# First cross-attention: denominators summed one step later from a deeper fold buffer, other work moved to other steps

## The chip, the cores and the metric

The kernel runs on one core of one Trainium2 chip. The metric is the device time of one execution in microseconds. Before the change it is 1993.03 us, the median of three runs (1991.8 to 1994.41).

The core has engines that run their own queues in order and wait for each other by semaphores: TensorE (PE; its weight loads are PEld), VectorE (DVE), ScalarE (ACT), GpSimd (POOL) and SyncE (SP, which here issues the transfers).

## The reference, cut to what matters

Two layers, each a gated cross-attention and a gated feed-forward part, over x of 4 batches x 1024 tokens x 256 and a context of 4 x 77 x 256. All the edits are in the first of the four stages:

```python
x = x + jnp.tanh(g_xattn[0]) * _L0_xattn_ref(_layernorm(x, axis=-1), ctx_1024, ctx_1024, wq, bq, wk, bk, wv, bv, wo, bo)

def _L0_xattn_ref(q, k, v, wq, bq, wk, bk, wv, bv, wo, bo):   # 16 heads of 16
    qh = (q @ wq.T + bq) ...; kh = (k @ wk.T + bk) ...; vh = (v @ wv.T + bv) ...
    attn = softmax(einsum('bhqd,bhkd->bhqk', qh * SCALE, kh), axis=-1)
    out = einsum('bhqk,bhkd->bhqd', attn, vh)
    return out.reshape(B, Nq, C) @ wo.T + bo
```

The later stages (ternary feed-forward, second cross-attention, self-attention with top-3 gating) are the same code before and after.

## The kernel before

`first_attention` works on tiles of 128 tokens. There are 32 of them (T) and 16 pairs (n, two tiles), four pairs to a batch. Every engine walks through the same list of steps, `for T in STEPS` with T from -12 to 34, and in each step issues its share in an order written out by hand. Nothing else sets the order: an engine that waits holds back all that it has still to issue.

For a tile the work passes through the engines so:

- TensorE, step T-2: scores (L414), after the shift of the tile before it has read them.
- VectorE, step T-2: negative row maximum (L754, `row_max`) and shift (L769, `shift`).
- ScalarE, step T-2: exponential (L564, `exp`), in odd steps behind the evacuation of a query (L528).
- GpSimd, step T-2: `fold` adds each row of probabilities in three halvings, `half_sum` (L624), `quarter` (L626), `eighth` (L630). `eighth` has two buffers; the third halving waits for VectorE's reciprocal of two tiles before.
- VectorE, step T-1: `recip_sum` adds the ten numbers that remain per head (L776) and takes the reciprocal (L777). It waits for `eighth` of its tile.
- GpSimd, step T: `widen` copies the reciprocals to the width of a head, two copies (L639), ring of four (`r_wide`).
- TensorE, step T: transposes of the probabilities (L425) in groups of 4, 4 and 2.

Two tiles on, in odd step 2n+1, TensorE transposes the widened reciprocals of pair n-1 (`reciprocals`, L400), when `widen` has been done 2n times (tiles 0 to 2n-1), and the residual of an earlier pair is done (`d_fin`). It does this behind the scores and the first group of transposes of the step. Behind it in the same step come the other two groups, the query projection (L385), the output matmuls of pair n-1, second half (L445), and in steps 3, 11 and 19 keys and values of the next batch (L341, L349). In even steps TensorE does the scores, the transposes, those of x (L373), the output matmuls of the first half (L445) and the output projection (L462). ScalarE evacuates the transposed reciprocals (L570), VectorE multiplies the outputs by them (`weigh`, L762) in the next even step and later adds the residual (L790).

GpSimd has more in its queue, in this order in step T: at T % 8 == 0 the inverse square roots of the layer norm of the next batch (`root`, L609 to L98, 15 small instructions, each waited for), at T % 8 == 1 the offset (L617, L618), `fold(T + 2)`, `widen(T)`, in odd steps the output bias (`add_bias`, L647), at (T + 1) % 8 == 0 the V blocks (`block_v`, L659, five instructions), and, at the steps in `CHUNK_STEPS`, one of 22 pieces of the feed-forward weights, rounded (`round_chunk`, L652). VectorE collects the bits of the same piece in the same step (`mantissas`, L801). A piece's buffer (four of them) is filled again by SP when both are through with it; SP's loop asks for pieces by the same list. Ahead of its loop GpSimd made ones, waited for the V bias and the output bias from memory (`s_wide`), and multiplied to get the V bias over a whole tile (`vb_wide`, L685), which TensorE uses in step -1 (`v_bias`) and VectorE then in `whole_bias` (L783, L784).

Of the kernel before, what the change touches and what calls it, by code (L numbers as in the profile page):

```python
# [8 lines left out]
ALU = mybir.AluOpType  # L9
ACT = mybir.ActivationFunctionType  # L10
AX = mybir.AxisListType

P = 128
# [5 lines left out]
RSQRT_MAGIC = 0x5F3759DF  # L19
WCH = 1024  # L20
STAGE = 4
CHUNK_STEPS = (-5, -4, -2, -1, 1, 3, 4, 5, 6, 7, 9, 11, 12, 13, 15, 17, 19, 20, 21, 23, 25, 27)
MANTISSA = 0x7FFFFF


# [39 lines left out]
def spread(ap, dim, n):  # L65

    shape = list(ap.shape)
    shape[dim] = n
    return ap.broadcast_to(shape)
# [31 lines left out]
def first_attention(nc, ident, gates, gates_src, x_src, x_dst, ctxT, wqT, wkT, wvT, woT, bias, H, ffn, head, tag):  # L101

    B, _, S = ctxT.shape
    HD = wqT.shape[1]
    dh = HD // H
    C = HD // P
# [6 lines left out]
    HALF = -(-S2 // 8) * 4  # L113
# [5 lines left out]
    RS = 4  # L119
# [25 lines left out]
    with semaphores(nc, tag) as sem, ExitStack() as ctx:  # L145
        def sb(name, shape, dt=F32):
            return ctx.enter_context(nc.sbuf_tensor(f"{tag}_{name}", shape, dt))
# [9 lines left out]
        kbias = sb("kbias", [P, C])  # L157
        kb_masked = sb("kb_masked", [P, C, HR])
        vbias = sb("vbias", [P, C])
        ones = sb("ones", [P, P])  # L160
        vb_wide = sb("vb_wide", [P, C, P])
        obias = sb("obias", [P, D])
        kt = sb("kt", [P, 2, C, HR, S])
# [14 lines left out]
        prob_all = sb("prob", [P, PR, KC * P])  # L178
        half_sum = sb("half_sum", [P, H, HALF])
        quarter = sb("quarter", [P, H, HALF // 2])  # L180
        eighth = sb("eighth", [P, 2, H, HALF // 4])
        negmax = sb("negmax", [P, H])
        rsum = sb("rsum", [P, RS, H])
        r_wide = sb("r_wide", [P, RS, H, dh])
# [46 lines left out]
        def _(sp):  # L231
# [63 lines left out]
            store_v(0)  # L295
            for i in range(2, STAGE):
                load_chunk(i)
            for dst, src in ((vbias[:, :], bv.rearrange("(c p) -> p c", p=P)),
                             (obias[:, :], spread(bo.rearrange("(a n) -> a n", a=1), 0, P))):
                sp.dma_start(dst, src, allow_slow_non_contiguous=True).then_inc(s_wide, 16)  # L300
            load_w(3, wo, woT)
            load_x(PB + 2)
            load_x(PB + 3)
# [298 lines left out]
        def _(pool):  # L602
# [17 lines left out]
            def fold(T):  # L620
                pool.wait_ge(a_exp, T + 1)
                if T:
                    pool.wait_ge(p_eighth, T)
                own.step(pool.tensor_tensor(half_sum[:, :, 0:S2 // 2], prob[:, T % PR, :, 0:S2 // 2],  # L624
                                            prob[:, T % PR, :, S2 // 2:S2], ALU.add))
                own.step(pool.tensor_tensor(quarter[:, :, :], half_sum[:, :, 0:HALF // 2],  # L626
                                            half_sum[:, :, HALF // 2:HALF], ALU.add))
                if T >= 2:
                    pool.wait_ge(d_r, T - 1)
                pool.tensor_tensor(eighth[:, T % 2, :, :], quarter[:, :, 0:HALF // 4],  # L630
                                   quarter[:, :, HALF // 4:HALF // 2], ALU.add).then_inc(p_eighth, 1)

            def widen(T):
                pool.wait_ge(d_r, T + 1)
                if T >= RS:
                    pool.wait_ge(e_r, (T - RS) // 2 + 1)
                by_place = rsum[:, T % RS, :].rearrange("p (g c j) -> p c g j", c=C, j=HR)
                for c in range(C):
                    ins = pool.tensor_copy(r_wide[:, T % RS, HC * c:HC * (c + 1), :].rearrange("p (g j) w -> p g j w", j=HR),  # L639
                                           spread(by_place[:, c, :, :].unsqueeze(3), 3, dh))  # L640
                ins.then_inc(p_wide, 1)
# [37 lines left out]
                own.link(pool.affine_select(out=v_mask[:, i, :], in_=v_mask[:, i, :], compare_op=ALU.is_ge, fill=0.0,  # L679
                                            base=S - 1 - P * k + SEG * m, pattern=[[S2, HR]], channel_multiplier=-1))  # L680
            own.wait()
            own.step(pool.memset(ones[:, :], 1.0))
            pool.wait_ge(s_wide, 32)
            for c in range(C):
                ins = pool.tensor_tensor(vb_wide[:, c, :], ones[:, :], spread(vbias[:, c:c + 1], 1, P), ALU.mult)  # L685
            ins.then_inc(s_vb, 1)
            pool.wait_ge(s_pad, 1)
            pool.wait_ge(root_done, 1)
            for T in STEPS:
                n, odd = divmod(T, 2)  # L690
                if T % 8 == 0 and 1 <= (T + 8) // 8 <= B:
                    root((T + 8) // 8)
                if T % 8 == 1 and 1 <= (T + 8) // 8 <= B:
                    offset((T + 8) // 8)
                if 0 <= T + 2 < TILES:
                    fold(T + 2)
                if 0 <= T < TILES:
                    widen(T)
                if odd and 0 <= n < NP:
                    add_bias(n)  # L700
                if (T + 1) % 8 == 0 and 0 <= (T + 1) // 8 < B:
                    block_v((T + 1) // 8)
                if T in CHUNK_AT:
                    round_chunk(CHUNK_AT[T])

        @block.vector
        def _(dve):
# [64 lines left out]
            def recip_sum(T):  # L772
                dve.wait_ge(p_eighth, T + 1)
                if T >= RS:
                    dve.wait_ge(p_wide, T - RS + 1)
                own.step(dve.tensor_reduce(rsum[:, T % RS, :], eighth[:, T % 2, :, :], AX.X, ALU.add))  # L776
                dve.reciprocal(rsum[:, T % RS, :], rsum[:, T % RS, :]).then_inc(d_r, 1)  # L777

            def whole_bias():
# [46 lines left out]
            for T in STEPS:  # L826
                n, odd = divmod(T, 2)
                if not odd and 0 <= n - 2 < NP:
                    weigh(n - 2)
                if 0 <= T + 2 < TILES:  # L830
                    row_max(T + 2)
                if 0 <= T + 2 < TILES:
                    shift(T + 2)
                if 0 <= T + 1 < TILES:
                    recip_sum(T + 1)
                if T in CHUNK_AT:
                    mantissas(CHUNK_AT[T])
                if T == CHUNK_STEPS[-1] + 1:
                    mantissa_found()
                b, p = divmod(T + 12, 8)  # L840
                if p < PB and 0 <= PB * b + p < NP + HEAD:
                    ln_stats(PB * b + p)
                if T == -1:
                    whole_bias()
                if not odd and 0 <= n - 2 < NP:
                    residual(n - 2)
                if T == TILES:
                    judge()
# [1902 lines left out]
def laid_out(inputs):  # L2751

    import numpy as np

    def cols(v):
        return v.reshape(-1, P).T

    a = {}
    for name, v in inputs.items():
        v = np.asarray(v)  # L2760
        if name == "x":
            a[name] = v.reshape(-1, v.shape[-1])
        elif name == "ctx_1024":
            a["ctxT"] = v.transpose(0, 2, 1)
        elif name.startswith("L0_xattn_w") or (name.startswith("L0_ffn_") and name.endswith("_w")):
            a[name + "T"] = v.T
        elif name.endswith("Wkv"):
            half = v.shape[1] // 2
            a[name[:-3] + "Wk"], a[name[:-3] + "Wv"] = v[:, :half], v[:, half:]
        elif name in ("L0_xattn_bq", "L0_xattn_bk", "L1_xattn_ln_scale", "L1_xattn_ln_bias", "L0_ffn_w1_s",  # L2770
                      "L0_ffn_w2_s", "L0_ffn_h1_s", "L0_ffn_h2_s"):
            a[name] = cols(v)
        else:
            a[name] = v
    return {name: np.ascontiguousarray(v) for name, v in a.items()}
# [14 lines left out]
```

## Time and profile before

| what | value |
|---|---|
| profiled execution | 1992.12 us, span 1990.4 us from the first to the last instruction |
| median of three runs | 1993.03 us |
| mean granted TensorE clock | 0.978 |
| busy share of the span: PE, DVE, ACT, POOL | 93%, 60%, 55%, 37% |
| first attention | from 0 to about 250 us |
| the same shares from 175 to 200 us | PE 24.8, DVE 21.6, ACT 17.6, POOL 19.2 of 25 us |

Times in the rows are counted from the start of the span. L400 is line 400 of the kernel before. In a row of a timeline the first number is the start, the second the duration from there to the end of the last merged instruction, `x4` how many were merged, and the bracket how long the engine was idle before and what ended it. "issue" stands for idle time without a cause that the profile shows.

### The profile page before, as it was taken

How to read it: one execution, taken by the hardware profiler on the slowest of the kernel's cores; microseconds unless marked ns; L12 is line 12 of the kernel's file. 1: busy time of each engine (PE TensorE's matmuls, PEld its weight loads, DVE VectorE, ACT ScalarE, POOL GpSimd, SP SyncE). 2: the span in 40 equal slices, each digit the busy share in tenths (PEclk: the TensorE clock that was granted, in tenths of full speed). 3: DMA queues.
4: the chain of work that ended last, by engine and by line, in shares of the span. 5: the costliest groups of instructions: out<-in, count | busy, mean ns of one | idle time of the engine just before them, and what ended most of it. 6: DMA issues, size and time to landing. Idle time of an engine off the chain costs nothing. (4 is left out here: it accounts for less than half of the span.)

```text
span 1990.4 us, 60604 instructions
## 1 busy us (share of the span) xinstructions
PE 1845.3 (93%) x26589; PEld 1496.7 (75%) x26589; DVE 1184.3 (60%) x1654; ACT 1085.9 (55%) x1900; POOL 728.7 (37%) x1012
## 2 busy tenths in 40 slices
PE   6898779999999999998799987899999999999997
PEld 4666568787887878887678776788777887887875
DVE  7787522332323233242555543888888898888885
ACT  4666433443434344342455543677777777767763
POOL 6878601000010000000333331556655665656552
PEclk9999989999999999999799998999999999999999
DMA  5331000000000000000301004322332243223211
GB/s 178 99 101 56 23 27 1 22 21 1 22 1 22 22 1 22 0 22 12 110 28 44 30 22 118 87 66 63 93 104 58 60 109 93 61 62 109 78 51 35
DMA packets 147004, 106.23 MB, mean 53 GB/s; under 512 B 19992, under 2 KB 143152, under 8 KB 146736
## 3 DMA queue, kind: packets, MB, share of 16 engines
q1 hardware_dynamic: 146736, 102.28, 17.4%
q8 instruction: 215, 3.52, 0.7%
q14 instruction: 53, 0.43, 0.1%
HBM read 76.77 MB, written 25.49 MB: 51 GB/s over the span
## 5 line engine op out<-in xcount | busy, mean ns | idle before, releaser
L2264 ACT ACTIVATE E_prob<-E_ps_s,E_negmax 128x1024 f32<-128x1024 f32 x256 | 284.9, 1115 | 144.2 <-DVE E_negmax L2577 143.7
L2577 DVE TENSOR_REDUCE E_negmax<-E_ps_s 128x1 f32<-128x1024 f32 x256 | 301.4, 1219 | 82.6 <-PE E_ps_s L2084 82.2
L2584 DVE STREAM_TRANSPOSE E_prob<-E_prob 128x1024 f32<-128x1024 f32 x256 | 303.9, 1225 | 24.0 <-ACT E_prob L2264 11.5
L2103 PEld LDWEIGHTS E_ps_o<-E_prob,E_vrep 32*64 32x64 f32 x15872 | 231.1, 130 | 64.5 <-ACT E_part L2290 56.7
L2103 PE MATMUL E_ps_o<-E_prob,E_vrep 32*64 32x128 f32 x15872 | 262.5, 274 | 13.4 <-issue 3.9
L1690 ACT ACTIVATE F_raw<-F_ps,ffn_scales 128x512 f32<-128x512 f32 x128 | 88.3, 690 | 288.0 <-PE F_ps L1599 288.0
L1599 PE MATMUL F_ps<-F_ha,ffn_w_rounded 128*128 128x512 f32 x1024 | 240.7, 395 | 0.0
L1599 PE MATMUL F_ps<-F_hb,ffn_w_rounded 128*128 128x512 f32 x1024 | 240.2, 395 | 0.0
L1599 PEld LDWEIGHTS F_ps<-F_ha,ffn_w_rounded 128*128 128x128 f32 x1024 | 190.9, 188 | 48.4 <-issue 1.7
L1599 PEld LDWEIGHTS F_ps<-F_hb,ffn_w_rounded 128*128 128x128 f32 x1024 | 192.0, 188 | 46.9
L2480 POOL TENSOR_TENSOR E_part<-E_part 128x512 f32<-128x512 f32 x93 | 119.4, 1284 | 249.6 <-ACT E_part L2290 249.6
L1777 DVE TENSOR_TENSOR F_ha<-F_raw,F_ha 128x512 fp32r<-128x512 f32 x64 | 44.3, 692 | 184.2 <-ACT F_ha L1692 184.2
L1777 DVE TENSOR_TENSOR F_hb<-F_raw,F_hb 128x512 fp32r<-128x512 f32 x64 | 44.3, 692 | 169.2 <-ACT F_hb L1692 169.2
L1599 PE MATMUL F_ps<-F_xt_part,ffn_w_rounded 128*128 128x512 f32 x512 | 126.7, 407 | 10.7 <-POOL F_xt_part L1711 4.7
L95 POOL TENSOR_TENSOR F_rs<-F_rs 128x4 f32<-128x4 f32 x24 | 4.8, 199 | 337.5 <-DVE F_rs L1742 336.2
L2084 PE MATMUL E_ps_s<-E_k_hi,E_q_hi 64*128 64x512 f32 x512 | 114.4, 442 | 14.9 <-ACT E_prob L2264 13.5
L1599 PEld LDWEIGHTS F_ps<-F_xt_part,ffn_w_rounded 128*128 128x128 f32 x512 | 96.2, 194 | 39.0 <-DVE F_raw L1767 8.8
L1711 POOL TENSOR_TENSOR F_xt_part<-F_xt,F_xt_part 128x1024 fp32r<-128x1024 f32 x8 | 19.2, 2399 | 272.0 <-ACT F_xt_part L1658 163.9
L2084 PE MATMUL E_ps_s<-E_k_hi,E_q_lo 64*128 64x512 f32 x512 | 102.4, 393 | 0.0
L2084 PE MATMUL E_ps_s<-E_k_lo,E_q_hi 64*128 64x512 f32 x512 | 101.3, 390 | 0.0
L1767 DVE SCALAR_TENSOR_TENSOR F_raw<-F_ps,ffn_scales,F_silu 128x512 f32<-128x512 f32 x64 | 47.7, 750 | 67.7 <-ACT F_silu L1674 67.7
L2084 PEld LDWEIGHTS E_ps_s<-E_k_hi,E_q_hi 64*128 64x128 f32 x512 | 48.0, 184 | 42.6 <-ACT E_prob L2264 23.5
(315 smaller groups left out, 3912.7 us busy)
## 6 DMA issues: line engine op xcount, KB each, us to landing
E_vrep<-E_v_all SPq DMA_DIRECT2D x128, 256.0 KB, 3.0
A_w_stage<-in_L_ffn_h_wT SPq DMA_DIRECT2D x16, 512.0 KB, 3.9
E_v_all<-E_vst SPq DMA_DIRECT2D x32, 256.0 KB, 2.2
C_x<-x SPq DMA_DIRECT2D x20, 256.0 KB, 6.7
F_x<-x SPq DMA_DIRECT2D x9, 512.0 KB, 3.7
A_x<-in_x SPq DMA_DIRECT2D x16, 256.0 KB, 5.5
x<-A_x SPq DMA_DIRECT2D x16, 256.0 KB, 2.2
x<-F_x SPq DMA_DIRECT2D x8, 512.0 KB, 2.9
```

The lines of the kernel that those rows point to most:

```text
L95: own.step(eng.tensor_tensor(t, y, y, ALU.mult))
L1599: mm = pe.matmul(out, fw.chunk(w, name, k, j * P, (j + 1) * P), a[:, k, :], start=k == 0 and i == 0, stop=k == K - 1 and i == len(parts) - 1)
L1690: act.activation(raw[:, u % 2, :], ps[:, u % 4, :], ACT.Gelu, scale=scale).then_inc(u_raw, 1)
L1711: pool.tensor_tensor(xt_part[1][:, :, :], xt[:, :, :], xt_part[0][:, :, :], ALU.subtract).then_inc(xt_lo, 1)
L1767: dve.scalar_tensor_tensor(out=dst, in0=ps[:, 2 * (j % 2) + 1, :], scalar=scales[:, 1, j:j + 1], in1=silu[:, j % 2, :], op0=ALU.mult, op1= ...
L1777: dve.tensor_tensor(dst, raw[:, u % 2, :], hi, ALU.subtract).then_inc(u_lo, 1)
L2084: mm = pe.matmul(ps_s[:, j, keys], a[rows, c % 2, cols], k[rows, c % 2, keys], start=i == 0, stop=i == 2)
L2103: mm = pe.matmul(low[64 * j:64 * j + 64, g, :], vrep[rows, slot, KB // 4 * (quarter % 2) + k, dh * j:dh * (j + 1)], prob[rows, u % 2, :, j ...
L2264: act.activation(prob[:, s // UT % 2, s % UT, j, :], ps_s[:, j, :], ACT.Exp, bias=negmax[:, at:at + 1], scale=1.0, accum_out=den[:, 2 * c ...
L2480: pool.tensor_tensor(part[:, 0, :], part[:, 0, :], part[:, 1, :], ALU.add).then_inc(part_added, 1)
L2577: dve.tensor_reduce(negmax[:, at:at + 1], ps_s[:, j, :], AX.X, ALU.max, negate=True).then_inc(d_max, 1)
L2584: dve.transpose(at, at).then_inc(d_t, 1)
```

## The change

- `recip_sum(T)` is issued by VectorE in step T, it was in step T-1. `eighth` has three buffers and the third halving waits for the reciprocal of three tiles before.
- `widen(T - 1)` is issued by GpSimd in step T, it was `widen(T)`. TensorE's code, `reciprocals` included, is not in the diff.
- The V blocks are made at (T + 2) % 8 == 0, one step earlier.
- `CHUNK_STEPS` is a new list: after -5 and -4 come 1 to 6, 9 to 14, 18 to 22 and 26 to 28; steps -2, -1, 7, 15, 17, 23 and 25 have no piece any more.
- `whole_bias` is issued by VectorE in step 0 behind the maximum and the shift, it was at the end of step -1.
- `ones` is gone; the V bias is spread by copies in GpSimd's step -3, and the wait for `s_wide` is there now. The V bias is laid out on the host as columns, so that its load is contiguous.

```diff
--- before.py
+++ after.py
@@ -19,7 +19,7 @@
 RSQRT_MAGIC = 0x5F3759DF
 WCH = 1024
 STAGE = 4
-CHUNK_STEPS = (-5, -4, -2, -1, 1, 3, 4, 5, 6, 7, 9, 11, 12, 13, 15, 17, 19, 20, 21, 23, 25, 27)
+CHUNK_STEPS = (-5, -4, 1, 2, 3, 4, 5, 6, 9, 10, 11, 12, 13, 14, 18, 19, 20, 21, 22, 26, 27, 28)
 MANTISSA = 0x7FFFFF
 
 
@@ -157,7 +157,6 @@
         kbias = sb("kbias", [P, C])
         kb_masked = sb("kb_masked", [P, C, HR])
         vbias = sb("vbias", [P, C])
-        ones = sb("ones", [P, P])
         vb_wide = sb("vb_wide", [P, C, P])
         obias = sb("obias", [P, D])
         kt = sb("kt", [P, 2, C, HR, S])
@@ -178,7 +177,7 @@
         prob_all = sb("prob", [P, PR, KC * P])
         half_sum = sb("half_sum", [P, H, HALF])
         quarter = sb("quarter", [P, H, HALF // 2])
-        eighth = sb("eighth", [P, 2, H, HALF // 4])
+        eighth = sb("eighth", [P, 3, H, HALF // 4])
         negmax = sb("negmax", [P, H])
         rsum = sb("rsum", [P, RS, H])
         r_wide = sb("r_wide", [P, RS, H, dh])
@@ -295,9 +294,9 @@
             store_v(0)
             for i in range(2, STAGE):
                 load_chunk(i)
-            for dst, src in ((vbias[:, :], bv.rearrange("(c p) -> p c", p=P)),
+            for dst, src in ((vbias[:, :], bv),
                              (obias[:, :], spread(bo.rearrange("(a n) -> a n", a=1), 0, P))):
-                sp.dma_start(dst, src, allow_slow_non_contiguous=True).then_inc(s_wide, 16)
+                sp.dma_start(dst, src).then_inc(s_wide, 16)
             load_w(3, wo, woT)
             load_x(PB + 2)
             load_x(PB + 3)
@@ -625,9 +624,9 @@
                                             prob[:, T % PR, :, S2 // 2:S2], ALU.add))
                 own.step(pool.tensor_tensor(quarter[:, :, :], half_sum[:, :, 0:HALF // 2],
                                             half_sum[:, :, HALF // 2:HALF], ALU.add))
-                if T >= 2:
-                    pool.wait_ge(d_r, T - 1)
-                pool.tensor_tensor(eighth[:, T % 2, :, :], quarter[:, :, 0:HALF // 4],
+                if T >= 3:
+                    pool.wait_ge(d_r, T - 2)
+                pool.tensor_tensor(eighth[:, T % 3, :, :], quarter[:, :, 0:HALF // 4],
                                    quarter[:, :, HALF // 4:HALF // 2], ALU.add).then_inc(p_eighth, 1)
 
             def widen(T):
@@ -679,11 +678,6 @@
                 own.link(pool.affine_select(out=v_mask[:, i, :], in_=v_mask[:, i, :], compare_op=ALU.is_ge, fill=0.0,
                                             base=S - 1 - P * k + SEG * m, pattern=[[S2, HR]], channel_multiplier=-1))
             own.wait()
-            own.step(pool.memset(ones[:, :], 1.0))
-            pool.wait_ge(s_wide, 32)
-            for c in range(C):
-                ins = pool.tensor_tensor(vb_wide[:, c, :], ones[:, :], spread(vbias[:, c:c + 1], 1, P), ALU.mult)
-            ins.then_inc(s_vb, 1)
             pool.wait_ge(s_pad, 1)
             pool.wait_ge(root_done, 1)
             for T in STEPS:
@@ -694,14 +688,19 @@
                     offset((T + 8) // 8)
                 if 0 <= T + 2 < TILES:
                     fold(T + 2)
-                if 0 <= T < TILES:
-                    widen(T)
+                if 0 <= T - 1 < TILES:
+                    widen(T - 1)
                 if odd and 0 <= n < NP:
                     add_bias(n)
-                if (T + 1) % 8 == 0 and 0 <= (T + 1) // 8 < B:
-                    block_v((T + 1) // 8)
+                if (T + 2) % 8 == 0 and 0 <= (T + 2) // 8 < B:
+                    block_v((T + 2) // 8)
                 if T in CHUNK_AT:
                     round_chunk(CHUNK_AT[T])
+                if T == -3:
+                    pool.wait_ge(s_wide, 32)
+                    for c in range(C):
+                        ins = pool.tensor_copy(vb_wide[:, c, :], spread(vbias[:, c:c + 1], 1, P))
+                    ins.then_inc(s_vb, 1)
 
         @block.vector
         def _(dve):
@@ -773,7 +772,7 @@
                 dve.wait_ge(p_eighth, T + 1)
                 if T >= RS:
                     dve.wait_ge(p_wide, T - RS + 1)
-                own.step(dve.tensor_reduce(rsum[:, T % RS, :], eighth[:, T % 2, :, :], AX.X, ALU.add))
+                own.step(dve.tensor_reduce(rsum[:, T % RS, :], eighth[:, T % 3, :, :], AX.X, ALU.add))
                 dve.reciprocal(rsum[:, T % RS, :], rsum[:, T % RS, :]).then_inc(d_r, 1)
 
             def whole_bias():
@@ -831,8 +830,10 @@
                     row_max(T + 2)
                 if 0 <= T + 2 < TILES:
                     shift(T + 2)
-                if 0 <= T + 1 < TILES:
-                    recip_sum(T + 1)
+                if T == 0:
+                    whole_bias()
+                if 0 <= T < TILES:
+                    recip_sum(T)
                 if T in CHUNK_AT:
                     mantissas(CHUNK_AT[T])
                 if T == CHUNK_STEPS[-1] + 1:
@@ -840,8 +841,6 @@
                 b, p = divmod(T + 12, 8)
                 if p < PB and 0 <= PB * b + p < NP + HEAD:
                     ln_stats(PB * b + p)
-                if T == -1:
-                    whole_bias()
                 if not odd and 0 <= n - 2 < NP:
                     residual(n - 2)
                 if T == TILES:
@@ -2767,7 +2766,7 @@
         elif name.endswith("Wkv"):
             half = v.shape[1] // 2
             a[name[:-3] + "Wk"], a[name[:-3] + "Wv"] = v[:, :half], v[:, half:]
-        elif name in ("L0_xattn_bq", "L0_xattn_bk", "L1_xattn_ln_scale", "L1_xattn_ln_bias", "L0_ffn_w1_s",
+        elif name in ("L0_xattn_bq", "L0_xattn_bk", "L0_xattn_bv", "L1_xattn_ln_scale", "L1_xattn_ln_bias", "L0_ffn_w1_s",
                       "L0_ffn_w2_s", "L0_ffn_h1_s", "L0_ffn_h2_s"):
             a[name] = cols(v)
         else:
```

## Rows read from the trace of the kernel before

**Rows 1.** Windows: busy us of each engine (instructions), granted clock, DMA share, GB/s.
```profile
49.40:228.30 178.90, 160.03 (x1464) 112.57 (x1463) 137.56 (x190) 107.83 (x199) 143.45 (x229) 0.96 0.25 73
```

**Rows 2.** Waits, 0 to 255 us: who waited for whom: us, times, longest.
```profile
DVE A_rsum L776 <- POOL A_eighth L630: 30.4, 14, 6.4
...
POOL A_vb_wide L685 <- DMA A_obias<-in_L_xattn_bo: 14.1, 1, 14.1
```

**Rows 3.** Timeline, TensorE: start, us, engine, line, operation, count [idle before <-releaser].
```profile
132.05 0.60 PE L400 MATMUL A_ps_m<-ident,A_r_wide 128*128 128x128 f32 x4
...
138.89 1.50 PE L445 MATMUL A_ps_o<-A_pt,A_v_blk 128*32 128x256 f32 x18
...
142.24 0.81 PE L414 MATMUL A_ps_s<-A_kt,A_q 32*128 32x154 f32 x16
...
143.47 0.60 PE L400 MATMUL A_ps_m<-ident,A_r_wide 128*128 128x128 f32 x4
```

**Rows 4.** Timeline, ScalarE and GpSimd beside rows 3.
```profile
130.77 1.03 POOL L652 CAST ffn_w_rounded<-A_w_stage 128x1024 fp32r<-128x1024 f32 x1
...
131.77 1.52 POOL L624 TENSOR_TENSOR A_half_sum<-A_prob 128x624 f32<-128x624 f32 x1
...
134.75 0.52 POOL L639 COPY A_r_wide<-A_rsum 128x128 f32<-128x128 f32 x2
...
136.21 1.23 ACT L564 ACTIVATE A_prob<-A_prob 128x1232 f32<-128x1232 f32 x1
...
137.52 1.53 POOL L624 TENSOR_TENSOR A_half_sum<-A_prob 128x624 f32<-128x624 f32 x1 [2.25 <-ACT A_prob L564]
...
140.50 0.53 POOL L639 COPY A_r_wide<-A_rsum 128x128 f32<-128x128 f32 x2
...
141.29 1.23 ACT L564 ACTIVATE A_prob<-A_prob 128x1232 f32<-128x1232 f32 x1 [1.63 <-DVE A_prob L769]
...
142.22 1.69 POOL L659 TENSOR_TENSOR A_v_blk<-A_v_k,A_v_mask 128x160 f32<-128x160 f32 x5
```

**Rows 5.** Timeline over the inverse roots, then a window (columns of rows 1).
```profile
144.98 0.24 POOL L609 TENSOR_SCALAR A_rs<-A_mv 128x8 f32<-128x8 f32 x1
...
149.41 1.52 POOL L624 TENSOR_TENSOR A_half_sum<-A_prob 128x624 f32<-128x624 f32 x1
...
152.37 0.53 POOL L639 COPY A_r_wide<-A_rsum 128x128 f32<-128x128 f32 x2
...
154.84 2.59 PE L445 MATMUL A_ps_o<-A_pt,A_v_blk 128*32 128x256 f32 x18 [4.45 <-issue]
...
159.82 0.81 PE L414 MATMUL A_ps_s<-A_kt,A_q 32*128 32x154 f32 x16
...
155.00:157.00 2.00, 2.00 (x18) 0.84 (x10) 1.97 (x2) 0.00 (x0) 1.84 (x3) 0.52 0.04 8
```

**Rows 6.** Timeline, four places: a slow rounding, step 11, its fold, a bit collection.
```profile
75.04 2.04 POOL L652 CAST ffn_w_rounded<-A_w_stage 128x1024 fp32r<-128x1024 f32 x1
...
106.64 0.60 PE L400 MATMUL A_ps_m<-ident,A_r_wide 128*128 128x128 f32 x4
...
118.07 2.19 POOL L624 TENSOR_TENSOR A_half_sum<-A_prob 128x624 f32<-128x624 f32 x1 [0.26 <-ACT A_prob L564]
...
135.36 1.16 DVE L801 TENSOR_TENSOR A_w_bits<-A_w_bits,A_w_stage 128x1024 int32<-128x1024 int32 x1
```

**Rows 7.** Timeline at the start of the stage, and step 29.
```profile
30.22 1.53 POOL L624 TENSOR_TENSOR A_half_sum<-A_prob 128x624 f32<-128x624 f32 x1 [1.07 <-ACT A_prob L564]
...
32.76 1.43 DVE L754 TENSOR_REDUCE A_negmax<-A_ps_s 128x16 f32<-128x1232 f32 x1
...
48.11 0.81 PE L414 MATMUL A_ps_s<-A_kt,A_q 32*128 32x154 f32 x16 [1.98 <-DVE A_prob L769]
...
49.41 1.06 PE L400 MATMUL A_ps_m<-ident,A_r_wide 128*128 128x128 f32 x4
...
228.29 0.63 PE L400 MATMUL A_ps_m<-ident,A_r_wide 128*128 128x128 f32 x4 [1.25 <-DVE A_x L790]
```

## The prediction

> **What bounds the kernel now.** I read the windows first. The change sits in the first attention, which ends near 250 us; in its steady part TensorE is busy 160 of 179 us [rows 1], so TensorE sets the pace, and the other engines matter where they make it stand still. The list of waits says where: VectorE stood 30.4 us before the sum of denominators until GpSimd had made `eighth` [rows 2]. The timeline then gives the beat. I call X the start of the transposes of the reciprocals (L400), which TensorE does once in each odd step. A pair of steps undisturbed is 11.42 us from X to X (132.05 to 143.47), with no idle time noted [rows 3]. Three pairs are longer by about 6 us: GpSimd's queue holds the inverse square roots of the next batch (4.43 us, 144.98 to 149.41) between one fold and the next; VectorE, which wants that fold at once, stands up to 6.4 us [rows 2]; behind it stands TensorE, 4.45 us, waiting for the weighted outputs that VectorE makes next [rows 5]. The first X is at 49.41, the fourteenth (step 29) at 228.29: 178.88 us for 13 pairs [rows 7].
>
> **The change, part by part.**
>
> VectorE's sum moves from step T-1 to T. It then asks for a fold that is a step old, so the 30.4 us of waiting go. Taken alone that would give back the three stalls (4.45 us and the slow matmuls behind each). A third `eighth` buffer covers the later read; it costs nothing: the wait of GpSimd for the buffer was never last.
>
> GpSimd's widening moves from T to T-1 too, and this is the part I take to decide. In each GpSimd step the order is: fold(T+2), widening, bias. TensorE's L400 in odd step 2n+1 wants the widened reciprocals of tile 2n-1. Before, those are made in GpSimd's step 2n-1, behind fold(2n+1). Now they are made in step 2n, behind fold(2n+2), and TensorE's code isn't changed. In the pair shown, L400 of step 17 starts at 143.47 and its widening (tile 15) began at 140.50 [rows 3, 4]. The slot that this widening gets now is the one at 152.37 [rows 5]. Even in step 15, where nothing special is queued, L400 started at 132.05 and the new slot is at 134.75 [rows 3, 4]. TensorE would stand in every odd step, with the transposes of the probabilities, the query projection, the output matmuls and the next scores queued behind it. What follows makes this a loop, so the lateness isn't paid once but in every pair:
>
> - X to the exponential of the next odd tile: L400 at 132.05, exponential at 136.21, fold of that tile at 137.52: 5.47 us [rows 3, 4]. (ScalarE evacuates the query ahead of it, so L400 and the projection are in front.)
> - this fold, its widening, the bias, up to the next thing in GpSimd's queue: 137.52 to 142.22, 4.70 us [rows 4].
> - a weight piece in an odd step: 130.77 to 131.77, 1.00 us [rows 4]. In an even step it falls into GpSimd's gap ahead of the next odd fold, as do the V blocks (now in an even step, five instructions, 1.7 us) and the offset.
> - fold and widening of the even tile: 131.77 to 134.75 and 0.52 for the two copies, 3.50 us [rows 4], and some 0.1 to wake TensorE.
>
> Sum: 13.77 us for a plain pair, 14.77 with an odd piece, against 11.42. The even exponential is not the limit: it starts at 141.29, ends 10.5 us after X with TensorE undisturbed [rows 3, 4], and its chain without VectorE's old wait is shorter still. With the roots it is 13.77 + 4.43 = 18.20; against 17.58 before (scores of one odd step to those of the next, 142.24 to 159.82 [rows 3, 5]): the stall isn't removed, it changes its waiter. Where TensorE also makes keys and values (steps 3, 11, 19) the even exponential comes later: its fold began 11.43 us after X (106.64 to 118.07 [rows 6]), so 11.43 + 3.50 + 0.1 = 15.03.
>
> Between step 3 and step 29 that is: 3 x 15.03 (steps 3, 11, 19), 5 x 14.77 (5, 9, 13, 21, 27), 3 x 18.20 (7, 15, 23), 2 x 13.77 (17, 25) = 201.1 us against 178.9: **+22.2**.
>
> Start. GpSimd no longer stands 14.1 us for the bias load [rows 2]; the pieces are rounded earlier and the broadcast of the V bias goes to step -3. VectorE no longer has a piece, a sum and the output bias before the third row maximum (32.76 [rows 7]), which can start about 2.5 us earlier. But GpSimd's own queue decides again. Fold(1) cannot begin before 30.22 [rows 7] (its exponential follows the same projection), it needs 3.0; then roots 4.4, fold(2) 3.0, offset 1.3, fold(3) 3.0, one widening 0.5, bias 1.25, piece 1.0, fold(4) and widening 3.5: X of step 3 at about 51.6 instead of 49.41: **+2.2**. From both sides: -2.5 if VectorE's gain comes through, +4 if each link is a little late. The contiguous bias load, the removed multiply by ones (two instructions of 0.4) and the SP queue (pieces are asked for at other steps, V rows behind them, wanted two steps later) I put at nothing; the gap of GpSimd covers them, and uncovered they cost 1 us each, once. End: the last bit test of the weights leaves the road of one pair, **-0.4**.
>
> Two costs the sum doesn't hold yet. **The clock.** After 4.45 us of idle the granted clock is 0.52 in the window behind it, near the lower of its two levels, and from the end of the idle time to the next scores it took 4.98 us (154.84 to 159.82 [rows 5]) instead of 3.35 (138.89 to 142.24 [rows 3]): 1.64 lost. After 1.98 us of idle L400 takes 1.06 instead of 0.60 [rows 7, 3], so idle of 2 us can do it as well; after 1.25 us it takes 0.63 [rows 7]. The new idle times are 2.35 (plain), 3.35 (piece) and about 7 us (steps 3, 9, 17, 25), and what slows lies on the loop. Four at 1.64 make 6.6; the other nine between 0 and 1.64, I take the middle, 7.4: **+14.0**, bounds +6.6 and +21.3. **VectorE against GpSimd.** When VectorE's bit collection (L801, 1.16 us alone) fell in an even step, GpSimd's work beside it grew: half sum 2.19 for 1.52, rounding 2.04 for 1.03 [rows 6, 4]. All four even pieces between steps 4 and 28 did this (0.37 to 1.01, mean 0.68); no odd one made GpSimd slower. After the change ten are even between steps 4 and 28, and now GpSimd's queue is the bound: **+6.8**, bounds 0 and +10. The Trainium skill, "SBUF — State Buffer", on the shared port pair, says that a VectorE operation with two SBUF inputs and a GpSimd operation that reads SBUF exclude each other for a whole instruction; by that rule, full exclusion would give up to 10 x 1.16 = 11.6; the rows show the mean of 0.68, and the trace agrees as to which operations suffer.
>
> Total: 22.2 + 2.2 - 0.4 + 14.0 + 6.8 = +44.8. The profiled execution took 1992.12 us (span 1990.4), the median is 1993.03, so they can stand for each other: 1992.1 + 44.8 = **2036.9 us**. The stages behind are not touched; they start later by the same amount.
>
> **Rivals.**
>
> *The change does what it looks like (faster).* If the widening came in time, TensorE would run its 11.42 beat through the root steps: three pairs of 17.58 become 11.42, and the start gives 2.5: 1992.1 - 18.5 - 2.5 = 1971. For it: the wait of VectorE is real and is removed. It decides if the widening of tile 2n-1 ends before L400 wants it, which needs an even fold 3.2 us earlier than at 131.77, while its exponential isn't done by then. 4 in 100.
>
> *The stall moves but the loop closes elsewhere (about even).* If the odd fold ran ahead of the query evacuation and the pieces and the bias fell in gaps, the loop would be the one through the scores, VectorE and the even exponential. That starts 9.24 us after X in the pair shown [rows 3, 4], some 1 us of it behind VectorE's statistics and old wait (an estimate): 8.2, exponential 1.3, fold and widening 3.5, 0.1: 13.1 per pair, with roots that hide half: 13 x 13.1 + 3 x 2.2 + 2.2 - 178.9 = 0.2, with the clock's 6.6: 1999 (range 1988 to 2010). Against it: the order in ScalarE's queue is fixed. 5 in 100.
>
> *No added cost (2016 at least).* Loop as forecast, clock and VectorE cost little: 1992.1 + 24.0 = 2016, up to 2026 with half of the clock's share. 28 in 100.
>
> *TensorE's clock.* The Trainium skill, "TensorE: Matmul & The Clock Gate", section "HAM oscillation", has a pattern where idle time in each turn makes each turn start at the lower clock. As a mechanism here: every L400 runs at 1.2 GHz, all nine middle pairs lose 1.64 as after 154.84, and all collisions cost 1.0: 24.0 + 21.3 + 10 = +55, 2047 us; beyond it lies 2055 if the even steps lose too. 15 in 100. The rows so far show the drop behind 1.98 and 4.45 us, none behind 1.2.
>
> **How the numbers follow.** Forecast (2026 to 2044) 48 in 100, little added cost (2016 to 2026) 28, all added 15, about even 5, faster 4. The range leaves out the two last and the top of the third: 2015 to 2049. A measurement of this kernel can tell 0.2% (4 us) from no change. Faster 0.05, the same 0.03, slower 0.92.
>
> **What would show it.** Right: the waits list TensorE at L400 (or its weight load) behind the widening L639, some fourteen times, 2 to 7 us each, 45 to 60 us in all; VectorE no longer waits for `eighth`; X to X is 13.8 to 15.5, and about 18 over the roots; the granted clock of the stage is lower. Wrong: X to X at 11.4 and no wait at L400, then the order I read in GpSimd's queue is mistaken; or X to X near 13.1 with the pieces free; or L624 no longer than 1.52 and the clock at 1.00, then the added costs fall away and 2016 stands.

## The result and the profile after

The changed kernel takes 2049.65 us (median of four runs, 2047.89 to 2051.54) against 1992.41 us before: ratio 1.0293, 95% interval 1.0278 to 1.0308. It is 57 us slower. The forecast was slower, 2036.9 us, with a range up to 2049; the measured time lies 0.65 us above it. The profiled execution has a span of 2046.2 us against 1990.4.

The waits in the first attention of the kernel after (who waited for whom, us in total, times, longest). Line numbers are lower by one than before: L399 are the transposes of the reciprocals, L638 is the widening, L623 the half sum, L800 the bit collection, L563 the exponential.

```profile
DVE A_o L761 <- PE A_ps_o L444: 91.9, 16, 10.5
POOL A_half_sum L623 <- ACT A_prob L563: 81.7, 19, 7.3
ACT A_r_t L569 <- PE A_ps_m L399: 75.9, 16, 9.3
PEld A_ps_m L399 <- POOL A_r_wide L638: 68.6, 15, 9.5
PE A_ps_m L399 <- POOL A_r_wide L638: 64.6, 14, 9.3
```

The wait of VectorE for `eighth`, 30.4 us before [rows 2], is gone. In its place TensorE waits for the widening, fourteen times, 64.6 us. GpSimd waits 81.7 us for exponentials, 30.0 in the same view before: it sits in the same loop, idle in one part and late in the other.

The window from step 3 to step 29 (busy us of PE, PEld, DVE, ACT, POOL; granted clock; DMA share; GB/s):

```profile
52.70:286.60 233.90, 175.98 (x1463) 127.17 (x1463) 136.27 (x189) 108.91 (x196) 149.22 (x228) 0.86 0.20 59
```

The same matmuls as in [rows 1] (1463 here, 1464 recorded there) take 233.9 us instead of 178.9; the granted clock is 0.86 instead of 0.96. The first attention holds the whole loss: the feed-forward stage has its first product at 320.55 instead of 261.53, 59.0 us later, and from there to the end the profiled execution is 3.2 us shorter, which no edit explains and which is within what executions differ by (17 of the kernel before on one chip lie between 1984.3 and 1994.1 us).

The loop, in the pair that ends at 159.16 (timeline, start and duration):

```profile
148.94 1.51 POOL L623 TENSOR_TENSOR A_half_sum<-A_prob 128x624 f32<-128x624 f32 x1 [4.54 <-ACT A_prob L563]
...
151.62 1.23 ACT L563 ACTIVATE A_prob<-A_prob 128x1232 f32<-128x1232 f32 x1 [0.54 <-DVE A_prob L768]
...
155.62 1.51 POOL L623 TENSOR_TENSOR A_half_sum<-A_prob 128x624 f32<-128x624 f32 x1
...
158.57 0.53 POOL L638 COPY A_r_wide<-A_rsum 128x128 f32<-128x128 f32 x2
...
159.16 1.11 PE L399 MATMUL A_ps_m<-ident,A_r_wide 128*128 128x128 f32 x4 [4.10 <-POOL A_r_wide L638]
```

The exponential of the even tile is over at 152.85; the fold that wants it starts at 155.62, since GpSimd's queue isn't there before. TensorE starts 0.06 us after the widening ends. In [rows 3] nothing stood ahead of L400.

X to X of the 13 pairs, by the step they start in, from the starts of L400 or L399 (us); the last row is the kernel with both costs taken away ("Both" below), for later:

| step | 3 | 5 | 7 | 9 | 11 | 13 | 15 | 17 | 19 | 21 | 23 | 25 | 27 | sum |
|---|---|---|---|---|---|---|---|---|---|---|---|---|---|---|
| before | 15.50 | 12.74 | 11.59 | 17.40 | 13.98 | 11.43 | 11.42 | 17.59 | 13.98 | 11.42 | 11.42 | 17.58 | 12.83 | 178.9 |
| forecast, without the two added costs | 15.03 | 14.77 | 18.20 | 14.77 | 15.03 | 14.77 | 18.20 | 13.77 | 15.03 | 14.77 | 18.20 | 13.77 | 14.77 | 201.1 |
| after | 17.95 | 15.69 | 21.72 | 18.48 | 16.88 | 15.70 | 20.26 | 17.88 | 17.05 | 15.69 | 20.65 | 18.08 | 17.81 | 233.8 |
| e8_fill_narrow | 15.36 | 14.67 | 18.25 | 14.71 | 15.07 | 14.68 | 18.26 | 14.05 | 15.01 | 14.67 | 18.25 | 14.05 | 15.20 | 202.2 |

### The profile page after: what moved, and what is told of

It reads as the page before. It is cut to its first block and busy times, and to the rows that moved or that the text cites. A ratio compares the mean times of both kernels' runs of the same rounds, so it can differ in the third digit from the quotient of the medians.

```text
span 2046.2 us, 60602 instructions
## 1 busy us (share of the span) xinstructions
PE 1856.7 (91%) x26589; PEld 1507.5 (74%) x26589; DVE 1184.2 (58%) x1654; ACT 1088.1 (53%) x1900; POOL 738.6 (36%) x1011
## 5 line engine op out<-in xcount | busy, mean ns | idle before, releaser
L623 POOL TENSOR_TENSOR A_half_sum<-A_prob 128x624 f32<-128x624 f32 x32 | 51.2, 1599 | 82.0 <-ACT A_prob L563 81.7
```

## The experiments

The theory: GpSimd's widening reaches TensorE one even fold too late, this alone closes the slow loop, and TensorE's clock and VectorE's bit collection make each turn longer. The rival: the moved pieces, V blocks and biases have a share. Each time is compared with the kernel before on the same chip (1987.75 us for the first four, 1988.75 for the next four, 1989.00 for the last two).

**The lag alone.** The kernel before with only the sum at T, three buffers and the later widening:

```diff
-        eighth = sb("eighth", [P, 2, H, HALF // 4])
+        eighth = sb("eighth", [P, 3, H, HALF // 4])
...
-                if 0 <= T < TILES:
-                    widen(T)
+                if 0 <= T - 1 < TILES:
+                    widen(T - 1)
...
-                if 0 <= T + 1 < TILES:
-                    recip_sum(T + 1)
+                if 0 <= T < TILES:
+                    recip_sum(T)
```

> The kernel before, with only the lag: sum at T, widen(T - 1), three fold buffers; pieces, V blocks and biases where they were. Theory: the lag alone makes the whole loss and a little more than the full change, since all odd steps have a piece on the loop and the V blocks stand ahead of the roots: 13 pairs of 211 us at full clock against 201, so 2050 to 2065. Rival (the moves share the blame): 1995 to 2035.

2048.88 us, ratio 1.0316 (1.0297 to 1.0335). The waits of this kernel:

```profile
PE A_ps_m L400 <- POOL A_r_wide L639: 71.1, 14, 10.3
```

The lag alone makes a loss as large as the full change. The time lies 1 us under the expected range. The 13 pairs sum to 237.4 us, 3.5 more than in the kernel after: the roots with V blocks and a piece ahead of them are longer (24.3, 23.2 and 22.9 us a pair), but the bit collections stretch the copies of the widening by 3.5 us only, 9.1 in the kernel after.

**The moves alone.** The kernel after with both at their old steps:

```diff
-                if 0 <= T - 1 < TILES:
-                    widen(T - 1)
+                if 0 <= T < TILES:
+                    widen(T)
...
-                if 0 <= T < TILES:
-                    recip_sum(T)
+                if 0 <= T + 1 < TILES:
+                    recip_sum(T + 1)
```

> The kernel after, with both VectorE's sum and the widening at their old steps; the moves of pieces, V blocks, V bias and output bias stay. Theory: GpSimd's queue ahead of the root steps is 2.7 us shorter (V blocks 1.7, piece 1.0), so each of the three stalls shrinks from 6.4 to 3.7 us on VectorE, TensorE stands 1.8 us and loses less to the clock; with 2.5 us at the start 1975 to 1986. Rival (the moves cost time, through collisions of the bit collection with GpSimd in even steps): 1992 to 2005.

1979.04 us, ratio 0.9957 (0.9942 to 0.9971): 9 us faster. The longest wait of VectorE for `eighth` is down from 6.4 us [rows 2] to 4.5 (3.7 were expected):

```profile
DVE A_rsum L775 <- POOL A_eighth L629: 22.5, 15, 4.5
```

So the rival falls: the moves gain where the lag is absent.

**The widening back at T.** The kernel after, VectorE's later sum kept, one line changed:

```diff
-                if 0 <= T - 1 < TILES:
-                    widen(T - 1)
+                if 0 <= T < TILES:
+                    widen(T)
```

> The kernel after, with widen(T) in step T again; VectorE's sum stays one step later. Theory (the widened reciprocals come one even fold too late for TensorE, and that alone closes the slow loop): TensorE no longer waits for the widening, and since VectorE doesn't wait for a fold either, the root steps cost nothing: pairs of 11.4 us throughout, 1971 us, 1965 to 1980. Rival (the moved pieces, V blocks and V bias have a part in the loss): it stays above the kernel before, 1995 to 2030. Second rival (GpSimd's queue over the roots still stops somebody): 1980 to 1992, with a wait of 2 to 4 us in each root step.

1972.29 us, ratio 0.9925 (0.9904 to 0.9946): 73 us under the changed kernel by the ratios of the two, from one line. The time is 1 us from the 1971 that was named, but that number was a gain of 21 us on 1992.1; against the kernel before on its own chip this one gains 15. The pairs are 11.4 to 12.1 us where neither a root nor keys and values are near, not 11.4 throughout: over the roots 12.3 to 13.8, with keys and values 14.0 to 14.3. The second rival has a small part: in four places TensorE still stood for the widening, 7.4 us in all, behind the first root of the loop 2.21 us:

```profile
97.66 0.66 PE L399 MATMUL A_ps_m<-ident,A_r_wide 128*128 128x128 f32 x4 [2.21 <-POOL A_r_wide L638]
```

**The widening of T-1, but ahead of roots and fold.** The same call moved up in GpSimd's step, its number unchanged.

> The kernel after, with widen(T - 1) still in step T, but ahead of the roots and the fold in GpSimd's queue. Theory (place in the queue decides, not the step's number): the same as with widen(T), 1965 to 1980, no wait of TensorE for the widening over 1 us. Rival (the number of the step decides, since the reciprocal itself is made too late): 2020 to 2050, with GpSimd waiting for VectorE's reciprocal.

1982.10 us, ratio 0.9980 (0.9969 to 0.9990). The expectation was too good: TensorE waits for the widening nine times, 18.1 us in all. Place does decide: 62 us are back with the number unchanged, and GpSimd doesn't wait for a reciprocal. But at the head of step T the widening stands behind all that step T-1 has at its end, which in the steps after a root is late:

```profile
102.28 1.26 POOL L646 TENSOR_TENSOR A_x<-A_x,A_obias 128x512 f32<-128x512 f32 x1
103.49 1.04 POOL L651 CAST ffn_w_rounded<-A_w_stage 128x1024 fp32r<-128x1024 f32 x1
104.47 1.52 POOL L638 COPY A_r_wide<-A_rsum 128x128 f32<-128x128 f32 x2
...
106.05 1.12 PE L399 MATMUL A_ps_m<-ident,A_r_wide 128*128 128x128 f32 x4 [4.71 <-POOL A_r_wide L638]
```

The bias and a piece, 2.2 us, stand between the fold and the widening, the copies take 1.52 us instead of 0.53, TensorE waits 4.71 us and its first matmuls are slow (1.12 instead of 0.66).

**The clock.** In the kernel after, TensorE does spare transposes in its idle time, in the steps where it stood 4 us or more. The wait for the widening is behind them:

```diff
                 if n:
                     pe.wait_ge(d_fin, n)
                 else:
                     pe.wait_ge(x_taken, 4)
+                for _ in range({0: 48, 2: 24, 3: 48, 4: 24, 6: 24, 7: 48, 8: 24, 10: 24, 11: 48, 12: 24, 13: 24}.get(n, 0)):
+                    pe.transpose(ps_m[:, 0:TOK], ident[:, :], ident[:, :])
+                pe.wait_ge(p_wide, 2 * n + 2)
```

> The kernel after, with 24 or 48 spare transposes of the identity (about 2.8 or 5.6 us at the higher clock) in TensorE's idle time ahead of the reciprocals, in the steps where it stood 4 us or more; they are overwritten by the reciprocals. Theory (part of the loss is TensorE's clock: from X to the next fold it took 6.7 to 7.9 us in ten of 13 pairs, 5.47 where TensorE had stood 1.5 us or less): from X to the fold is 5.5 in all pairs, granted clock of the stage near 1, some 20 us faster than the kernel after, 2028 to 2034. Rival (the clock is a companion, the longer way from X comes from the engines' order): no gain, 2047 to 2055.

2030.68 us, ratio 1.0215 (1.0198 to 1.0232), some 16 us under the kernel after. First the kernel after, behind 7.65 us of idle:

```profile
108.10 1.11 PE L399 MATMUL A_ps_m<-ident,A_r_wide 128*128 128x128 f32 x4 [7.65 <-POOL A_r_wide L638]
...
110.29 3.13 PE L384 MATMUL A_ps_m<-A_xt,A_wq 128*128 128x256 f32 x8
...
115.50 1.52 POOL L623 TENSOR_TENSOR A_half_sum<-A_prob 128x624 f32<-128x624 f32 x1 [6.96 <-ACT A_prob L563]
```

with the granted clock of these microseconds (columns as in the window above; 0.50 is the lower level):

```profile
108.00:111.50 3.50, 3.40 (x13) 3.20 (x14) 0.00 (x0) 1.47 (x3) 0.45 (x3) 0.50 0.00 0
```

and a root step of this experiment (L395 are the spare transposes, L401 the reciprocals, L625 the half sum):

```profile
166.23 5.40 PE L395 MATMUL A_ps_m<-ident 128*128 128x128 f32 x48
...
173.09 0.66 PE L401 MATMUL A_ps_m<-ident,A_r_wide 128*128 128x128 f32 x4 [1.45 <-POOL A_r_wide L640]
...
174.52 1.97 PE L384 MATMUL A_ps_m<-A_xt,A_wq 128*128 128x256 f32 x8
...
178.57 1.52 POOL L625 TENSOR_TENSOR A_half_sum<-A_prob 128x624 f32<-128x624 f32 x1 [5.04 <-ACT A_prob L565]
```

X to the next half sum is 5.48 us in this step 17; in the kernel after it was 7.40 in the step 9 shown and 7.57 in step 17. The projection takes 1.97 us, there 3.13 and 3.31. Eleven pairs have 5.4 to 5.5. In steps 3 and 9 it is still 7.73 and 6.79: there TensorE stood 4.08 and 2.42 us more behind the spare transposes. The 13 pairs sum to 217.9 instead of 233.8, so at least 15.9 us of the loss are the clock; the two steps that stayed slow keep 3.6 us more.

**The bit collection.** In the kernel after, VectorE's bit collection reads one column of pieces 1 to 21:

```diff
-                    dve.tensor_tensor(w_bits[:, :], w_bits[:, :], words, ALU.bitwise_or).then_inc(d_bits, 1)
+                    dve.tensor_tensor(w_bits[:, 0:1], w_bits[:, 0:1], words[:, 0:1], ALU.bitwise_or).then_inc(d_bits, 1)
```

> The kernel after, with the bit collection of pieces 1 to 21 on one column instead of 1024 (the test of the weights then sees only part of them). Theory (the bit collection of even and odd steps meets the widening, which costs GpSimd 9 us in all, and the half sum in the steps with keys and values, 2 us): widening 0.53 us everywhere, 9 to 13 us faster than the kernel after, 2037 to 2041. Rival (VectorE is off the loop, and the longer copies are a matter of the record): under 3 us.

2024.40 us, ratio 1.0178 (1.0161 to 1.0195): some 23 us under the kernel after, twice what I expected. What it does in the kernel after (VectorE beside GpSimd):

```profile
189.98 1.52 POOL L638 COPY A_r_wide<-A_rsum 128x128 f32<-128x128 f32 x2
190.07 1.27 DVE L800 TENSOR_TENSOR A_w_bits<-A_w_bits,A_w_stage 128x1024 int32<-128x1024 int32 x1
191.47 1.27 POOL L646 TENSOR_TENSOR A_x<-A_x,A_obias 128x512 f32<-128x512 f32 x1
...
195.65 1.60 POOL L638 COPY A_r_wide<-A_rsum 128x128 f32<-128x128 f32 x2
...
195.94 1.16 DVE L800 TENSOR_TENSOR A_w_bits<-A_w_bits,A_w_stage 128x1024 int32<-128x1024 int32 x1
```

and with one column, the same two widenings:

```profile
178.36 0.53 POOL L638 COPY A_r_wide<-A_rsum 128x128 f32<-128x128 f32 x2
...
183.03 0.52 POOL L638 COPY A_r_wide<-A_rsum 128x128 f32<-128x128 f32 x2
```

Two copies that take 0.53 us together take 1.52 and 1.60. VectorE is a step ahead: the piece of step 18 (190.07) hits the widening in GpSimd's step 17, the one of step 19 (195.94) that of step 18, twice in one pair. Of the nine stretched widenings seven were hit by a piece of an even step, two by one of an odd step (19 and 27). The miss in size has a reason that the runs show: shorter turns also left TensorE less idle. X to the half sum exceeds 5.47 us by 19.9 us in all in the kernel after, by 13.5 us here. The sum of the pairs is 214.2, 19.7 less.

**Both.** Spare transposes and the bit collection on one column.

> Both: spare transposes and the bit collection on one column (the test of the weights then sees only part of them). Theory (loop at the higher clock without collisions, as the sum of the prediction had it before its two added costs: pairs of 13.77, 14.77 and 18.20 us): 2015 to 2023. Rival (the two overlap, or a third cost is left): 2025 to 2035.

2009.36 us, ratio 1.0104 (1.0086 to 1.0122), 21 us slower than before; lower than I expected. The pairs (table above) sum to 202.2 us; the forecast without its two added costs had 201.1, and no pair is off by more than 0.43. Such a pair over a root ends so:

```profile
157.78 1.53 POOL L625 TENSOR_TENSOR A_half_sum<-A_prob 128x624 f32<-128x624 f32 x1
...
160.75 0.52 POOL L640 COPY A_r_wide<-A_rsum 128x128 f32<-128x128 f32 x2
...
161.33 0.66 PE L401 MATMUL A_ps_m<-ident,A_r_wide 128*128 128x128 f32 x4 [1.42 <-POOL A_r_wide L640]
```

The four kernels split their 13 pairs so (us, from the starts and ends in the timelines). The first part is TensorE's and ScalarE's and holds the clock, the second is GpSimd's and holds the collisions:

| kernel | X to the odd half sum | from there to the end of the even widening | to the next X | sum |
|---|---|---|---|---|
| after | 91.0 | 142.2 | 0.7 | 233.8 |
| e5_fill | 74.7 | 142.3 | 1.0 | 217.9 |
| e6_narrow_bits | 84.6 | 128.8 | 0.7 | 214.2 |
| e8_fill_narrow | 71.0 | 129.6 | 1.6 | 202.2 |

So the clock costs the changed kernel 20.0 us (91.0 less 71.0) and the collisions cost it 12.6 to 13.4 directly. Without the collisions the clock costs 13.7 (84.6 less 71.0): the other 6.3 us are a slow clock that the collisions bring about, since TensorE stands longer.

**A better version.** The kernel after with `widen(T)` behind roots and offset and ahead of the fold:

```diff
                 if T % 8 == 1 and 1 <= (T + 8) // 8 <= B:
                     offset((T + 8) // 8)
+                if 0 <= T < TILES:
+                    widen(T)
                 if 0 <= T + 2 < TILES:
                     fold(T + 2)
-                if 0 <= T - 1 < TILES:
-                    widen(T - 1)
```

> The kernel after, with widen(T), in GpSimd's queue behind the roots and the offset and ahead of fold(T + 2). Theory (with widen(T) behind the fold TensorE still stood 2.8, 2.2, 1.7 and 0.7 us for it at the start and behind the roots; the reciprocal is ready before the exponential that the fold wants, so ahead of the fold the widening costs nothing): these waits go, 1962 to 1969. Rival (GpSimd then waits for VectorE's reciprocal and every fold is late): 1972 to 1995.

1967.40 us, ratio 0.9892 (0.9875 to 0.9908), 21 us faster than before and 80 us faster than the changed kernel. TensorE's waits for the widening are down to 0.3 us, from 7.4 with the widening behind the fold. The reason that I expected is only half right. GpSimd never stands for a reciprocal, but it doesn't wait for an exponential either: from 50 to 215 us it has no idle time at all. The half sum at 90.41 (tile 10) adds an exponential that was over at 79.46, and the one at 89.65 is that of tile 12. The two copies go ahead of a fold of 3 us and hold it up by 0.5. VectorE pays some of it: it waits 9.2 us for `eighth`, 0.4 with the widening behind the fold. The 13 pairs are only 0.5 us shorter than there, and X of step 3 comes 2.4 us earlier (44.26 against 46.66):

```profile
78.23 1.23 ACT L563 ACTIVATE A_prob<-A_prob 128x1232 f32<-128x1232 f32 x1 [0.54 <-DVE A_prob L768]
...
89.65 1.23 ACT L563 ACTIVATE A_prob<-A_prob 128x1232 f32<-128x1232 f32 x1 [0.54 <-DVE A_prob L768]
89.93 0.53 POOL L638 COPY A_r_wide<-A_rsum 128x128 f32<-128x128 f32 x2
90.41 1.51 POOL L623 TENSOR_TENSOR A_half_sum<-A_prob 128x624 f32<-128x624 f32 x1
```

**The same without the moves.** The lag alone, with the widening at that place:

> The kernel before with the lag alone, but widen(T) behind roots and offset and ahead of fold(T + 2); pieces, V blocks and biases at their old steps. Theory (with the widening in time VectorE's later sum takes the root stalls away; the old pieces and V blocks ahead of the roots cost 2.7 us of queue each time, of which part comes through, and the start keeps its 14 us wait): between the best version (1967) and the kernel before (1989): 1970 to 1980. Rival (the moves are what gains, the lag nothing once the widening is right): 1984 to 1992.

1968.46 us, ratio 0.9886 (0.9860 to 0.9913), the same as with the moves. So the expectation that the moves were worth a few more us here was wrong: the later sum with the widening in that place gains all of it, and the moves gain only where VectorE still waits for the fold. Whether the widening ahead of the fold would gain without the later sum was not run.

**The changed kernel once more.**

> The kernel after once more, beside the kernel before on this chip, for the sum of shares: if stages behind the first attention are not touched, the loss is what its first stage shows, 56 to 60 us (ratio 1.028 to 1.030). Rival (something behind gains or loses by the shift): outside that.

2047.22 us, ratio 1.0280 (1.0251 to 1.0308); with the first measurement, 56 to 58 us.

## Why the prediction was right, and where it failed

- *The step that decides* (widening of tile 2n-1 behind fold(2n+2), TensorE's code unchanged): right. TensorE waits there fourteen times as said, 64.6 us where 45 to 60 were named, and one line takes it all back.
- *The loop and its terms*: right. With clock and bit collection out of the way its 13 pairs measure 202.2 us against 201.1. X to the half sum is 5.48 (5.47 said), the root adds 4.54 us between the folds (9.23 against 4.69; 4.43 said), an odd piece 0.98. The signs named for the kernel itself, 13.8 to 15.5 us a pair and about 18 over the roots, were too low: 15.7 to 18.5 and 20.3 to 21.7.
- *"VectorE against GpSimd", +6.8, bounds 0 and +10*: this is the step that failed. The collisions of the changed kernel cost 12.6 to 13.4 us on GpSimd and bring 6.3 us more of slow clock with them; without them the pairs are 19.7 us shorter. Instruction by instruction, beside the bit collections of steps 4 to 28 GpSimd's are 12.8 us longer in all. The ten even pieces make 8.8 of this, 0.88 each where I took 0.68: seven of them hit a widening, which costs 1.0. Odd pieces, which I put at nothing, make 4.0 (steps 9, 11, 19 and 27). That "no odd one made GpSimd slower" misreads the trace of before: there each of the three pieces of steps 9, 17 and 25 stretched the second instruction of the offset to 1.09 us (0.24 alone); the other odd ones cost GpSimd nothing.

```profile
98.56 1.16 DVE L801 TENSOR_TENSOR A_w_bits<-A_w_bits,A_w_stage 128x1024 int32<-128x1024 int32 x1
98.72 1.09 POOL L618 TENSOR_SCALAR A_rs<-A_rs 128x8 f32<-128x8 f32 x1
```

  A collision belongs to the new schedule. The bound should have been each of the 17 pieces of steps 4 to 28 at 1.16 us, 20 us (an estimate from those rows), not ten.
- *The clock*, +14.0 of +6.6 to +21.3: 20.0 measured, 13.7 once the collisions are away. That the second number meets the forecast is in part luck: a slow turn costs 1.2 to 2.4 us, not 1.64 at most, but three middle pairs (from steps 5, 13 and 21) were spared, where TensorE had stood 1.2 to 1.5 us and not the 2.35 or 3.35 that I counted with. What the term lacked is that TensorE stands longer with every collision.
- *Together* the two are 31.6 us (233.8 less 202.2), 20.8 forecast: the clock is 6.0 over its term, the collisions 5.8, and the spare transposes hold up the turns of `e8_fill_narrow` by 1.0 (its 1.6 against 0.7 in the third column of times). The gap from 44.8 to the 59.0 us at the start of the feed-forward stage is so: 10.8 for the two, 1.1 in the plain pairs, 1.1 at the start, and 1.1 at the end (+0.7 us from step 29 on instead of -0.4).
- *The start*: +2.2 said, 52.74 against 49.41 is +3.3. The links as listed add up to 51.3, not 51.6, so the working gives +1.9. With the bit collection on one column X is at 49.49 and, with spare transposes too, at 50.33. So 2.4 to 3.3 us, most or all of it, are collisions again: those of steps 1 to 3 stretched an instruction of the roots, a quarter sum (1.72 us, 0.87 alone) and a half sum (2.48 for 1.52).
- *The rivals*: the nearest was "TensorE's clock", 2047 to 2055, which had 15 in 100. Its collisions of 1.0 each are what the stretched widenings show; its clock is not quite right, since four of the 13 L399 were not slow (0.65 or 0.66 us) and three pairs lost nothing. Each of the ten slow turns began behind idle time of 4.1 us or more, as this rival has it. "Faster", -21 us, didn't happen, but it is what the later sum gives once the widening is in time: -15 behind the fold, -21 ahead of it. The pairs are then 16.5 and 17.0 us shorter (18.5 said), the start 2.8 and 5.2 (2.5 said). "The loop closes elsewhere" has nothing in the runs for it.
- *The range*: its top left out the upper part of that rival, beyond 2049. That the measured time is 0.65 us above it is chance, since the four runs differ by 3.65 us and the later measurement, 2047.22, lies below the top. That the sum is 13 us short is not.

## What to carry to other kernels

When a hand-written schedule moves a producer by a step, find the consumer that isn't in the diff and ask what now stands ahead of the producer in its queue; a step's number says little, the last instruction ahead of it says all. Two moves that look like one: with the later sum the kernel is 15 or 21 us faster, by where the widening stands; widening a tile late takes this away and costs 57 on top, and only the sum had a reason to move. And costs that are hidden on an engine with slack, such as two engines holding each other up, must be counted again for every instruction that the change puts on the path.

## What the runs showed of the hardware

- The bit collection, a VectorE operation with two SBUF inputs, holds up even a 0.29 us GpSimd copy for nearly its whole length: the pair of copies took 1.52 to 1.60 us instead of 0.53 beside the 1.16 to 1.27 us of the bit collection, and 0.52 once that read one column. This agrees with the Trainium skill, "SBUF — State Buffer", on the shared port pair. That some 13 us of such waits were worth 19.7 us of loop time was new to me.
- TensorE, at the upper of its levels (2.4 GHz, granted clock 1.00) in the pairs undisturbed, was granted 0.50 to 0.77 over the projection behind every idle time of 4.1 to 9.3 us in the 13 pairs of the changed kernel (L384 2.43 to 3.62 us instead of 1.97), and 0.50, which is 1.2 GHz, over the reciprocals in nine of these ten (L399 1.11 instead of 0.66). Behind 1.2 to 1.5 us it stayed at 1.00. In between the idle time alone does not tell: behind 2.42 us the projection took 2.68 us with the spare transposes, behind 2.80 us 1.96 with the widening back at T.
- With spare transposes in the gap eleven of 13 turns kept the upper level over the projection, three without them. They took 16 us off the time, though they compute nothing.
